# Output matmuls ahead of state-update matmuls in a chunked retention loop

## The reference, cut to what matters

```python
xn = _layernorm(x, axis=-1)
s  = _L0_attn_ref(xn, ...)            # retention, below
g  = _silu(_L0_ffn_ref(xn, ...))      # hidden 3072, int weights
return x + s * g

def step(S, qkv):                     # one chunk of one head
    qb, kb, vb = qkv
    attn    = jnp.einsum('bhid,bhjd->bhij', qb, kb) * D[None]
    o_intra = jnp.einsum('bhij,bhjd->bhid', attn, vb)
    o_inter = jnp.einsum('bhid,bhde->bhie', qb * cross_q, S)
    S_new   = gC * S + jnp.einsum('bhjd,bhje->bhde', kb * cross_k, vb)
    return (S_new, o_intra + o_inter)
```

## Time and profile before

| | us |
|---|---|
| median of three runs | 3268.88 |
| the three runs | 3268.88, 3272.93, 2957.08 |
| the profiled execution, whole | 2947.61 |
| its slowest core's span (core 1) | 2946.1 |
| spans of the eight cores | 2921.8 to 2946.1 |
| retention stages of core 1, eight together | 630.7 |

### The profile page before, as it was taken

One profiled execution on the slowest core, in us unless ns is written; L12 is line 12 of the kernel. 1 busy time (PEld: TensorE's weight loads), 2 busy tenths in 40 slices (PEclk: granted clock), 3 DMA queues, 4 the chain that ended last, 5 costly groups with the idle time before them and its releaser, 6 DMA issues. The chain is left out here.

```text
span 2946.1 us, 32662 instructions; the slowest of 8 cores (2921.8 to 2946.1 us)
## 1 busy us (share of the span) xinstructions
PE 2320.1 (79%) x10736; PEld 1037.3 (35%) x10736; DVE 837.4 (28%) x1989; ACT 764.8 (26%) x1532; POOL 443.1 (15%) x564
## 2 busy tenths in 40 slices
PE   1586959687379999999917778695963799999999
PEld 0232424233134444444413333242431334444444
DVE  3523233333223111111244242333332331121112
ACT  2434343433201111111034333434331111101110
POOL 2011030301400220021020211203014002201210
PEclk9797979788589999999957879697975899999999
DMA  9120020200593775575380202102006837746753
GB/s 196 42 31 27 2 53 4 46 13 12 98 157 93 86 73 89 117 72 57 115 180 27 35 24 22 36 1 49 10 13 108 156 104 73 78 93 107 72 54 118
DMA packets 296914, 202.16 MB, mean 69 GB/s; under 512 B 212144, under 2 KB 261424, under 8 KB 296624
## 3 DMA queue, kind: packets, MB, share of 16 engines
q0 software_dynamic: 234240, 96.50, 28.6%
q1 hardware_dynamic: 62512, 103.59, 11.2%
HBM read 254.45 MB, written 41.94 MB: 101 GB/s over the span
## 5 line engine op out<-in xcount | busy, mean ns | idle before, releaser
L936 PE MATMUL P<-xnT,wgu 128*128 128x512 bf16 x1536 | 350.4, 381 | 29.7 <-DMA wgu<-fuw 20.3
L947 PE MATMUL P<-xnT,wgu 128*128 128x512 bf16 x1536 | 347.2, 379 | 0.0
L963 PE MATMUL P<-wd_sb,hT 128*128 128x512 bf16 x1536 | 332.2, 379 | 6.7 <-DVE hT L992 6.7
L992 DVE TENSOR_TENSOR hT<-sg_sc,P 128x1024 bf16<-128x1024 bf16 x96 | 117.3, 1221 | 599.5 <-PE P L947 599.5
L842 PE MATMUL P<-wo_sb,ogl 128*128 128x512 bf16 x1024 | 239.3, 394 | 45.8 <-DVE ogl L863 44.3
L975 ACT ACTIVATE sg_sc<-P 128x1024 bf16<-128x1024 f32 x96 | 98.3, 1024 | 567.6 <-PE P L936 567.6
L630 DVE SCALAR_TENSOR_TENSOR S<-S,U_ps 128x512 bf16<-128x512 bf16 x240 | 154.3, 684 | 309.3 <-PE U_ps L587 309.2
L401 POOL TENSOR_TENSOR og_sb<-o_win,ggb 128x512 bf16<-128x512 bf16 x128 | 147.9, 1158 | 590.0 <-ACT o_win L673 589.8
L913 POOL DMA_DIRECT2D wgu<-fgw x92 | 80.5, 875 | 990.4 <-PE P L947 990.4
L572 PE MATMUL kt_ps<-id_sb,kT 128*128 128x128 bf16 x256 | 40.6, 249 | 237.7 <-ACT ktok L666 237.7
L936 PEld LDWEIGHTS P<-xnT,wgu 128*128 128x128 bf16 x1536 | 146.7, 98 | 226.2 <-issue 62.9
(11 more groups left out here) (94 smaller groups left out, 2294.5 us busy)
## 6 DMA issues: line engine op xcount, KB each, us to landing
wgu<-fgw POOLq DMA_DIRECT2D x96, 256.0 KB, 4.7
wgu<-fuw POOLq DMA_DIRECT2D x96, 256.0 KB, 5.3
ln_x<-x SPq DMA_DIRECT2D x32, 512.0 KB, 10.0
og_spill<-og_st SPq DMA_DIRECT2D x128, 128.0 KB, 1.7
ogl<-og_spill SPq DMA_DIRECT2D x128, 128.0 KB, 2.7
xc_sb<-x SPq DMA_DIRECT2D x32, 512.0 KB, 4.4
out<-o_sb SPq DMA_DIRECT2D x32, 512.0 KB, 5.6
wd_sb<-fdw POOLq DMA_DIRECT2D x48, 256.0 KB, 41.0
```

The source lines that it names most:

```text
L936: ins = te.matmul(fgps[:, n * 512:(n + 1) * 512], wgu[:, par * 1024 + k * 128: par * 1024 + (k + 1) * 128], G.xnT[:, k * T + tok0 + n * 51 ...
L947: ins = te.matmul(fups[:, n * 512:(n + 1) * 512], wgu[:, 2048 + par * 1024 + k * 128: 2048 + par * 1024 + (k + 1) * 128], G.xnT[:, k * T + ...
L963: ins = te.matmul(ps[:, n * 512:(n + 1) * 512], hT[:, k * 1024 + mc * 128:k * 1024 + (mc + 1) * 128], wd_sb[:, k * D + n * 512:k * D + (n ...
L992: ins = v.tensor_mul(out=hT[:, m * 1024:(m + 1) * 1024], in0=sg_sc[:, (m % 2) * 1024:(m % 2 + 1) * 1024], in1=fups[:, :])
```

## The change

In each pass of the chunk loop PE issues the output O before the state update U. The order of the passes' other parts stays. The waits move with the matmuls: the first output matmul no longer waits for the state, and each of the two state matmuls waits for its own half (the second wait is the old one, `2 * c`). The waits of U are as they were. No instruction is added or taken away, and no other engine's program changes. The passes now go og_tr(c - 3), O(c), U(c), at_kt(c + 2).

```diff
                     if c >= LAG:
                         og_tr(c - LAG)
+                    WG(te, sAT.h, b["at"] + c + 1)
+                    WG(te, sOE.h, b["oe"] + 2 * c - 2)
+                    ins = te.matmul(o_ps[:, par * 512:(par + 1) * 512],
+                                    atm[:, par * 128:(par + 1) * 128],
+                                    vtb[:, c * 512:(c + 1) * 512],
+                                    start=True, stop=(c == 0))
+                    if c > 0:
+                        for d in range(2):
+                            WG(te, sS.h, b["st"] + 2 * c + d - 1)
+                            ins = te.matmul(o_ps[:, par * 512:(par + 1) * 512],
+                                            qT[:, d * T + c * 128:d * T + (c + 1) * 128],
+                                            Sb[c % 2][:, d * 512:(d + 1) * 512],
+                                            start=False, stop=(d == 1))
+                    sTo.inc(ins)
                     WG(te, sKT.h, b["kt"] + c + 1)
                     for d in range(2):
                         WG(te, sS.h, b["st"] + 2 * c + d - 1)
...
                         sTu.inc(ins)
-                    WG(te, sAT.h, b["at"] + c + 1)
-                    WG(te, sOE.h, b["oe"] + 2 * c - 2)
-                    WG(te, sS.h, b["st"] + 2 * c)
-                    ins = te.matmul(o_ps[:, par * 512:(par + 1) * 512],
-                                    atm[:, par * 128:(par + 1) * 128],
-                                    vtb[:, c * 512:(c + 1) * 512],
-                                    start=True, stop=(c == 0))
-                    if c > 0:
-                        for d in range(2):
-                            ins = te.matmul(o_ps[:, par * 512:(par + 1) * 512],
-                                            qT[:, d * T + c * 128:d * T + (c + 1) * 128],
-                                            Sb[c % 2][:, d * 512:(d + 1) * 512],
-                                            start=False, stop=(d == 1))
-                    sTo.inc(ins)
                     if c + 2 < NCH:
                         at_kt(c + 2)
```

## The result

The changed kernel takes 0.957 of the time of the kernel before (95% interval 0.956 to 0.959), about 126 us less: its median is 2829.8 us over ten runs, its profiled execution 2825.8. My sum was 122 us less, 2826 us against the profiled execution. The number that I gave was another, 3147 us, since I laid the sum on the median of the three runs shown. The ten runs of the kernel before have a median of 3051.7 us and go from 2950 to 3273, the ten of the changed kernel go from 2823 to 3058.

What follows compares the result with a forecast made beforehand. Retention stages were taken as bound by a PE-ACT wait loop, once a pass. 0.95 us x 128 = 122 us off, other terms priced 0: 2826 from the profiled 2947.6, but 3147 given from the 3268.9 median; range 2800 to 3200.

Steps and rivals of the forecast that it cites:

- U leaves the loop: PE-ACT wait loop, once a pass: without U, 4.08 to 3.62 us at full clock, 5.30 to 4.45 at half.
- The clock's answer: PE clock in retention stages: denser passes cut the 1.2 GHz share from 0.60 to 0.30; 122 us gained.
- only U's own time: Rival: retention loop shortens but the share of passes at 1.2 GHz stays 0.60; 89 us gained, 3180; chance 0.22.
- The state becomes late: Rival: DVE's state outruns its 1.4 us slack, PE waits, gain within 2%; 0.12 shared with clock down; step priced 0.
- PE's room under ACT: U and scores fit on PE during ACT's 2.17 us, leaving 1.7 or 1.3 us idle; price 0.
- POOL at the head: Head of a stage: POOL's first product, after 16 loads, still ends before PE's first og_tr; price 0.
- DVE and POOL at once: DVE's updates L630 run while POOL multiplies; collisions cost POOL at most 0.16 us, DVE nothing.
- slower: Rival: ACT's copy and square slowed by DVE's PSUM reads; slower by 2% from 1.41 us on, 3328; chance 0.03.
- upper level: Whole-kernel run times of 3269 to 3273 us, 11% above the profiled execution, taken as base; chance 0.55.
- the likeliest case: U out of the PE-ACT loop with a faster clock: 111 to 154 us off; chance 0.62.

Runs made afterwards that it cites:

- the half move: Changed kernel's order with only the second U matmul behind O, the first still in front; 0.981 of the kernel before, 57 us less.
- the clock held: Extra idle identity transposes on PE ahead of its ktok wait: 14 in the kernel before, 0.972; 8 in the changed kernel, 0.946 of the kernel before.
- the repeat: The changed kernel run again unchanged; profiled execution 2837 us, the other five of six runs 2872 to 3171, no ratio.
- the transposes' wait: Odd chunks' key transposes given their own PSUM bank, so they wait for an earlier ktok: 0.979 on the order before, 0.927 on the changed order.

## Why the prediction was right in its working and wrong in its number

**U leaves the loop: right.** 3.62 and 4.45 us a pass were forecast, 3.59 and 4.45 are measured, down from 4.08 and 5.30. That the place of U does it, and not the wait that went with it, is shown by the run with the wait kept (3.70) and by the half move (3.82).

**The clock's answer: right in size, on a thin argument.** I took 0.30 of the passes at 1.2 GHz and PEclk 0.83; the eight stages show 0.76 to 0.89, mean 0.84. The rival "only U's own time", 89 us, is excluded by 126 +- 6. The split in the sum was 89 for U and 33 for the clock; with the clock held, the runs make it 65 and 85 of which 64 were had. The two overlap, since U is dearer at the half clock, so either split adds up. Two things in the argument did not hold. The density of a pass at the full clock was read from a window that took in matmuls of the pass ahead of it at its edge (15 records instead of 13): cut at its own transposes, the pass had 1.88 us of 4.08, 46%, and has 1.81 of 3.58 now, 51%, where I had 49% and 56%. And the line between two rows would give a small step for a small edit; the runs show a larger one: with one U matmul or one met wait more in a pass the mean PEclk of the stages is 0.72 and 0.74, with the whole move 0.84 (0.81 in the repeat). So that 0.30 came out was in part luck: the run with one wait more lies 25 us higher.

**The state becomes late: right, price 0.** S was to be ready 1.46 us after the copy starts; it is at 233.01 + 1.28 = 234.29, 1.46 after 232.83. A delay of 1.2 us was free, one of 2.3 was not, which fits the 1.4 us of slack.

**PE's room under ACT, POOL at the head, DVE and POOL at once: right.** PE's wait for ktok fell to 177.1 us, within the 150 to 190 given, and PE's og_tr shows no wait for POOL's product. The earlier trace rows could say little of DVE and POOL at once: in the kernel before an update L630 and a product ran at the same time in only about four of 120 passes. Now they do in nearly every pass, and L630 still takes 679 to 690 ns, the product 1149 to 1307, and the copy 585 to 586: the rival "slower" had no effect at all to stand on.

**The met waits: a term that I left out.** I wrote that U's wait is met and gave it the price 0. Each met wait costs 0.11 us at the full clock where it stands behind short transposes. It did no harm here only because O has two waits in front of it where U had two; the change dropped the third (the state's) from that place and put it between long matmuls. Kept, it would have cost 25 us.

**The number: wrong.** The step that failed is the last one: the base from which the 122 us were taken, "Two of three runs lie at the upper level, so this is the number that I give". The sum was made against the profiled execution, 2947.6, and held there to 4 us (2826 forecast; 2825.8 in the profiled execution, 2829.8 in the median). Carried to 3268.9 it became 3147, 317 us over the result. The runs show no upper level: the longer times of the kernel before are spread from 3014 to 3273 us. They are 7 of the 10 in the result and 4 of the 30 beside the experiments, and 3 of 10 for the changed kernel in the result; why they were so many in the first case is not shown, and three runs could not tell. So the changed kernel's median fell among its short times while the other's did not, which nothing in the prediction had weighed. It also assumed that the 122 us hold at either level, which is not shown. The range from 2800 to 3200 held the time only because it was drawn around two levels; the likeliest case's own range at the lower one, 2794 to 2837, would have done.

## What to carry to other kernels

Look for the loop between two engines that wait for each other, and take out of it whatever only stands in front; what is left in the loop can be added up from start to start before anything is run, and a further part of it can be worth more once the others are out (the transposes' wait 62 us ahead of the change, 90 behind it). Keep waits that are met anyway away from the matmul behind short transposes, if the loop goes over it: between the 512-column matmuls they cost nothing here. If the granted clock swings in a stage, a change in the loop can pay about twice its own time (129 us of which 65 were U's place) or little more than that, and a run with idle work in PE's gaps tells what the clock is worth. Before you carry a gain to a median, look at how the single times spread, and don't call two of three a level.

## What the runs showed of the hardware that I had not expected

- Transposes of the identity into an unread bank, 0.94 us in each pass's gap, brought the granted clock of the stages from 0.59 to 0.71 up to 0.96 to 1.00 and made the kernel 82 us faster. The Trainium skill, TensorE: Matmul & The Clock Gate, section Part 4: PE-mode transpose, says that the full clock does not engage for transposes, which don't count as busy in the same way; these runs show that they hold it.
- Little moves the clock: the stages have PEclk 0.74 on average (0.69 to 0.89) with passes of 3.70 us at the full clock, and 0.84 (0.76 to 0.89) with passes of 3.59; the repeat of the latter has 0.81.
- A wait that is already met costs 0.11 us in front of a matmul behind short transposes at the full clock (0.23, 0.34 and 0.44 us with two, three and four of them) and next to nothing at the half clock (passes of 4.41, 4.41 and 4.43 us), and 0.25 us pass from the end of ACT's ktok to U behind two waits.
- SP's stores of 128 KB land after 1.7 us in the median, but the four in a stretch in which a head's weights were being loaded took 5.6 us in the median, and the longest of all 9.3; two slots did not cover that, four did.
